# A two-direction Mamba block: direction 1's B taps read the projection in PSUM, every transpose goes through one bank, and ScalarE's state copy and two squares stand ahead of the square roots

## What is computed

```
o  = silu(dwconv3x3(lin1(x)))                    # 8 images, L = 256 positions
s  = o @ fc_in
for d in (0, 1):                                 # direction 1 works on the flipped sequence
    z, xBC, dt = split(s @ W_in[d])
    xBC = silu(causal_conv1d(xBC, 4 taps))       # xs, B, C of 16 channels each
    h_t = exp(-dt*A) * h_(t-1) + dt*xs_t (x) B_t # scan over the 256 positions
    y_t = h_t . C_t + D*xs_t
    y   = y * silu(z);  y = y * rsqrt(mean(y*y) + 1e-5) * norm_w
    out += y @ W_out[d]
o  = batchnorm(out @ fc_out);  x1 = sigmoid(conv4(o)) * x + x
... layer norm, causal attention, layer norm, top-2 of 8 experts, residual
```

## Time and profile before

| | |
|---|---|
| median of 3 runs | 89.81 us (89.72 to 90.68) |
| the profiled execution | 90.41 us |
| its span, first to last instruction | 88.6 us |
| outside the span | 1.81 us |
| TensorE / VectorE / ScalarE / GpSimd busy | 91% / 66% / 46% / 23% |
| TensorE's granted clock | full in all of the span |

### The profile page before, as it was taken

The page is one execution under the profiler, slowest core; times in us unless marked ns, Lnnn a source line. Parts: engine busy times, 40 slices in busy tenths (PEclk is TensorE's granted clock), DMA queues, the critical chain, the costliest instruction groups (busy, mean ns, idle before and its releaser), DMA issues.

```text
span 88.6 us, 1936 instructions
## 1 busy us (share of the span) xinstructions
PE 80.4 (91%) x734; PEld 52.3 (59%) x734; DVE 58.7 (66%) x153; ACT 40.6 (46%) x94; POOL 20.6 (23%) x31
## 2 busy tenths in 40 slices
PE   4899999999899999899489799999999899999790
PEld 1268775464665665346245566876756545789680
DVE  1149996999989999564644366529326969999210
ACT  4040297988738710567368762333753242001100
POOL 6050004998699107910000000000000000000000
DMA  2994000000000000000000000000000000001001
GB/s 19 367 435 167 0 0 0 0 0 0 7 0 4 0 7 0 4 7 0 0 0 0 0 0 7 0 0 0 0 7 0 0 0 0 0 7 33 30 0 59
DMA packets 1305, 2.57 MB, mean 29 GB/s; under 512 B 144, under 2 KB 784, under 8 KB 1296
## 3 DMA queue, kind: packets, MB, share of 16 engines
q1 hardware_dynamic: 1152, 2.31, 7.2%
q10 hardware_dynamic: 144, 0.14, 0.5%
HBM read 2.19 MB, written 0.26 MB: 28 GB/s over the span
## 4 chain that ended last, share of the span: by engine, by line
PE 52%; DVE 23%; ACT 12%; issue 6%; DMA 4%; ACTq 0%; DVEq 0%
PE banks L1006 7%; DVE lmat L1159 6%; DVE pre L1152 4%; DMA pa<-in_pa 4%; PE banks L675 3%; PE banks L929 3%; DVE conv L1090 3%; PE banks L974 3%; PE banks L754 2%; PE banks L581 2%; PE banks L692 2%; PE banks L913 2%; PE banks L897 2%; DVE lmat L1380 2%; PE banks L662 2%
## 5 line engine op out<-in xcount | busy, mean ns | idle before, releaser
L574 PE MATMUL banks<-warm 128*128 128x512 bf16 x36 | 10.9, 422 | 1.2 <-DVE warm L1072 1.2
L1159 DVE TENSOR_TENSOR_SCAN lmat<-banks,data 128x512 f32<-128x512 f32 x8 | 9.8, 1219 | 0.8 <-PE banks L675 0.7
L1006 PE MATMUL banks<-pa,lmat 128*128 128x128 f32 x56 | 6.8, 277 | 0.0
L1006 PEld LDWEIGHTS banks<-pa,lmat 128*128 128x128 f32 x56 | 6.5, 192 | 0.1
L574 PEld LDWEIGHTS banks<-warm 128*128 128x128 bf16 x36 | 3.4, 106 | 4.8 <-issue 1.4
L301 POOL TENSOR_TENSOR data<-pa,dt_dir 128x512 f32<-128x512 f32 x4 | 4.0, 1042 | 7.9 <-DVE da L1139 7.9
L1380 DVE TENSOR_TENSOR lmat<-banks,wtok 128x256 f32<-128x256 f32 (+1 forms) x12 | 5.5, 506 | 0.2
L974 PE MATMUL banks<-pd,h 32*128 32x256 f32 x32 | 5.2, 397 | 0.1
L1165 DVE TENSOR_TENSOR mmat<-banks,lmat 128x512 f32<-128x512 f32 x8 | 5.4, 669 | 0.0
L301 POOL TENSOR_TENSOR data<-pb,dt_dir 128x512 f32<-128x512 f32 x4 | 5.0, 1262 | 0.0
L510 ACT ACTIVATE data<-banks 128x384 f32<-128x384 f32 x8 | 3.4, 491 | 3.0 <-PE banks L913 2.9
(11 more groups left out here) (201 smaller groups left out, 178.2 us busy)
## 6 DMA issues: line engine op xcount, KB each, us to landing
pc<-in_pc SPq DMA_DIRECT2D x1, 962.5 KB, 5.8
pb<-in_pb SPq DMA_DIRECT2D x1, 446.0 KB, 3.9
pd<-in_pd SPq DMA_DIRECT2D x1, 336.0 KB, 6.2
x<-in_x SPq DMA_DIRECT2D x1, 256.0 KB, 3.2
out<-fin SPq DMA_DIRECT2D x4, 64.0 KB, 1.6
pa<-in_pa ACTq DMA_DIRECT2D x1, 133.5 KB, 3.4
```

What stands on the lines that cost most here:

```text
L574: pe.matmul(bank[scratch][:, :], warm[:, 0:P], warm[:, :], start=True, stop=True)
L1006: mm = pe.matmul(o, mix[:, k, e, :, :], packs["ident"], start=False, stop=(e == terms - 1))
L1159: dve.tensor_tensor_scan(lmat[:, i, :], dab_bank, data1[:, i, :, :].rearrange("p q t -> p (q t)"), 0.0, ALU.mult, ALU.add).then_inc(S["sca ...
```

## The change

- `raw_copy(2)` is gone. `tap(2, s)` reads projection 2 in PSUM bank 6, as `tap(0, s)` did with bank 2, and `raw` holds direction 1's C and z alone.
- Both directions are transposed into bank 1. `transposed(0)` waits for `raw_copy(3)`, and `transposed(1)` for direction 0's two turn copies.
- The six filler matmuls write bank 1 too, so they wait for these two turn copies. `skipped(0)`, the first writer of bank 6, also waits for the last tap.
- On ScalarE `state_copy(1, 0)` stands ahead of `rms(1)`, and `square(3)` ahead of `rms(2)`. On TensorE `mean_squares(3)` and `(4)` each stand one place further ahead of the mixer's matmuls.

```diff
-        raw = sb("raw", [P, DIRS, BH, L])
+        raw = sb("raw", [P, BH, L])
...
-        t_part = lambda d, bh: unit_bank[d][:, L * bh:L * bh + L]
+        t_part = lambda bh: unit_bank[1][:, L * bh:L * bh + L]
...
             def centre_tap(n):
                 if n == 3:
-                    act.wait_ge(S["raw_ready"], 2)
+                    act.wait_ge(S["raw_ready"], 1)
...
             centre_tap(0)
             centre_tap(2)
-            raw_copy(2)
...
             rms(0)
             square(1)
+            state_copy(1, 0)
             rms(1)
-            state_copy(1, 0)
             square(2)
             state_copy(1, 1)
+            square(3)
             rms(2)
-            square(3)
             square(4)
             rms(3)
             rms(4)
...
             def transposed(d):
                 pe.wait_ge(S["s1_ready"], d + 1)
-                pe.wait_ge(S["raw_ready"], d + 1)
+                if d == 0:
+                    pe.wait_ge(S["raw_ready"], 1)
+                else:
+                    pe.wait_ge(S["s1t_copied"], BH)
...
             def skipped(i):
                 pe.wait_ge(S["s1t_copied"], BH if u == 0 else BH * DIRS)
+                if u == 0:
+                    pe.wait_ge(S["tapped"], 2 * PAD)
...
             products(0)
-            pe.wait_ge(S["raw_ready"], DIRS)
+            pe.wait_ge(S["s1t_copied"], BH)
             keep_warm(6, 1)
...
+            mean_squares(3)
             mixer_out(0, 0)
-            mean_squares(3)
+            mean_squares(4)
             mixer_out(0, 1)
-            mean_squares(4)
             mixer_out(1, 0)
             keep_warm(1, 6)
             mixer_out(1, 1)
...
             def tap(n, s):
-                if n == 2:
-                    dve.wait_ge(S["raw_ready"], 1)
-                src = raw[:, 0, :, :] if n == 2 else proj[n]
+                src = proj[n]
```

More of the change, by code:

```diff
@@ L373, in centre_tap @@
                 if n == 3:
-                    act.wait_ge(S["raw_ready"], 2)
+                    act.wait_ge(S["raw_ready"], 1)
                 else:
                     act.wait_ge(S["proj_done"], PROJ_ORDER.index(n) + 1)
-                act.activation(pre[:, n, :, :], raw[:, 1, :, :] if n == 3 else proj[n], ACT.Copy,
+                act.activation(pre[:, n, :, :], raw[:, :, :] if n == 3 else proj[n], ACT.Copy,
                                scale=packs["tap_col"][:, TAPS1 * n + PAD:TAPS1 * n + TAPS1])\
@@ L382, in raw_copy @@
                 act.wait_ge(S["proj_done"], PROJ_ORDER.index(n) + 1)
-                act.activation(raw[:, n - 2, :, :], proj[n], ACT.Copy).then_inc(S["raw_ready"], 1)
+                act.activation(raw[:, :, :], proj[n], ACT.Copy).then_inc(S["raw_ready"], 1)
             def other_taps(n):
@@ L387, in other_taps @@
                     col = TAPS1 * n + PAD - s
-                    act.activation(tap3[:, s - 1, :, :], raw[:, n - 2, :, :], ACT.Copy,
+                    act.activation(tap3[:, s - 1, :, :], raw[:, :, :], ACT.Copy,
                                    scale=packs["tap_col"][:, col:col + 1]).then_inc(S["tap3_ready"], 1)
@@ L426, in turn_copy @@
                 act.wait_ge(S["s1t_done"], d + 1)
-                act.activation(s1t[:, d, NC * bh:NC * bh + NC, :, :].rearrange("p k q c -> p (k q c)"), t_part(d, bh),
+                act.activation(s1t[:, d, NC * bh:NC * bh + NC, :, :].rearrange("p k q c -> p (k q c)"), t_part(bh),
                                ACT.Copy).then_inc(S["s1t_copied"], 1)
@@ L643, in transposed @@
                 pe.wait_ge(S["s1_ready"], d + 1)
-                pe.wait_ge(S["raw_ready"], d + 1)
+                if d == 0:
+                    pe.wait_ge(S["raw_ready"], 1)
+                else:
+                    pe.wait_ge(S["s1t_copied"], BH)
                 for bh in range(BH):
                     for c in range(NC):
-                        mm = pe.transpose(t_part(d, bh)[:, Q * c:Q * c + Q], s1[:, d, bh, Q * c:Q * c + Q], packs["ident"])
+                        mm = pe.transpose(t_part(bh)[:, Q * c:Q * c + Q], s1[:, d, bh, Q * c:Q * c + Q], packs["ident"])
                 mm.then_inc(S["s1t_done"], 1)
```

## The result

The changed kernel took 89.9 us, the median of 21 executions (88.74 to 91.89), beside 90.52 us for the kernel before, run beside it (89.72 to 93.56, also 21). The ratio is 0.9889 (0.9856 to 0.9922), which at the 89.81 us shown is a gain of 1.00 us, to 88.8. The forecast was 88.7 with a range from 88.2 to 89.5, and the measured 89.9 lies above it. So the ratio bears out most of the gain, and the median does not: it lies 1.1 us above the ratio's time.

The account below looks back on a forecast made before the run. It took one dependent line across engines as the bound, with VectorE's taps bounding at 18 to 25 us. Terms 0.42 + 0.43 + 0.27 = 1.12 us, taken from 89.81, gave 88.7 us, range 88.2 to 89.5.

Parts of the forecast that it names:

- The taps at 0.75 each: VectorE's second three B taps, read from PSUM, take 0.75 us each, so scan(1) ends 0.95 us earlier.
- Place one: The stretch from 18 to 25 us, taps to decays(2): decays(2) starts 0.42 us earlier, TensorE-bound from there.
- place two: The stretch from 36 to 43 us, output_carry to last mixer matmul: 0.43 from state copy plus 0.27 us from squares.
- The fillers at 20.65, their new wait of no cost: TensorE's fillers before decays(2) still start at 20.65 us; their wait for the second turn copy costs 0.
- Rival A: Turn copies come late, fillers and decays(2) slip, and all 0.42 us is lost: 89.1 us, chance 0.12.
- The state copy 0.43: Moved ahead of rms(1) on ScalarE, it lets output_carry start without its wait: 0.43 us (0.39 to 0.47).
- the squares and mean squares 0.27: At the last roots, their new order brings the last normed piece and mixer matmul 0.27 us further forward.
- Rivals B: At the roots, late gated(3) holds rms(2); 0.27 and half of 0.43 us go: 89.2 us, chance 0.10.
- C: The PSUM source makes the taps longer, up to 1.405 us each, delaying scan(1): 90.1 us, chance 0.04.
- The copy removed ... is worth 0: Removing one 0.58 to 0.60 us copy from ScalarE gains 0, since ScalarE sits idle later anyway.
- the distance from it to the end unchanged: From the last mixer matmul to the kernel's end, everything moves along with no change in length.
- Rival D: TensorE's clock falls to 1.2 of 2.4 GHz between 30 and 44 us, adding 2 us: 90.7, chance 0.02.

Follow-up runs that it names:

- e4_lock: Kernel before, taps still from SBUF, with one added wait holding GpSimd's fifth step until the last B tap is over; ratio 0.9923.
- e2_taps: Changed kernel without the edits to the roots: taps from PSUM, one transpose bank and new waits alone; ratio 0.9967 to the kernel before.
- e5_state: Kernel before with only the state copy moved ahead of rms(1); ratio 0.9929.
- e3_roots: Kernel before with state copy, square(3) and mean squares moved as in the change; taps, banks and waits as before; ratio 0.9914.
- e8_spare: Changed kernel plus a 128x1 ScalarE copy into an unread tile where the removed copy stood; median 90.88 us of 6, no ratio.
- e13_before_late: Kernel before with three extra matmuls on unused data among the last four experts; median 93.81 us, ratio 1.0373.
- e11_late: Changed kernel with a spare ScalarE copy, four fillers instead of six, and three extra matmuls among the last four experts; median 95.25 us.
- e12_thin: Changed kernel with a spare ScalarE copy, four fillers instead of six, and two instead of six unused matmuls ahead of the last four experts; ratio 0.9804.

## Why the prediction was right in most of its parts and wrong in its number

- **The taps at 0.75 each.** Right: 2.29 us for three, GpSimd's instruction 1.04. The reading that the excess was a wait for GpSimd, taken from three end times, was borne out by e4_lock for all three taps. The surplus for a PSUM source that the Trainium skill gives (VectorE: DVE Perf Modes, the errata table) would have been, as an estimate from that table, 65 ns a tap; with GpSimd out of the way the two sources took 747 and 748 ns, so the trace doesn't agree here. The Trainium skill's advice that the prediction names, to copy to SBUF first where many operations follow (VectorE: DVE Perf Modes, "Rules for kernel authors"), is what the kernel before did, and it met what the Trainium skill's exclusion rule (SBUF — State Buffer, "SBUF: two separate sides") describes: e4_lock agrees with that rule, since a tap that began beside a GpSimd step ended 0.55 us behind the step's end and the taps without one took 748 ns.
- **Place one at 0.42 (0.35 to 0.51).** TensorE-bound from there on, as said, and without a wait ahead of decays(2). Measured 0.53, 0.59 and 0.53 with place two, and 0.41 alone; counted from the fillers' start, which takes out its own noise, 0.51 to 0.52 in all four (1.82 less 1.30 or 1.31), at the upper end. The step that was mis-sized is "decays(2) can start between 21.96 and 22.12; I take 22.05". In the trace after decays(2) starts 1.30 us behind the fillers' start, 0.17 ahead of their modelled end, where I had taken 1.40 and 0.07; before, an idle time stood behind the fillers, so this couldn't be read there.
- **The fillers at 20.65, their new wait of no cost.** Right: counted from the first tap they start at 6.00 after and at 6.01 before, and where they start at 6.11 (e2_taps) so they do in e5_state, which has the old wait. Rival A, that this wait eats the gain, fell.
- **The state copy 0.43, the squares and mean squares 0.27.** Right, the best two terms: e5_state gives 0.46 and e3_roots 0.26 more; both and 0.05 of interplay make 0.77. Rivals B and C fell.
- **"The copy removed ... is worth 0".** Wrong, and with it "the distance from it to the end unchanged". It cost 0.30 us at the gate, 30 us later; a spare instruction in its place takes that back (e8_spare), and with it moves a transfer of instructions from the gate to 35.25 us. How the one does the other isn't shown. This is the one term that was put at nothing and cost time; the sum would have been 0.42 + 0.43 + 0.27 - 0.30 = 0.82. Since the terms before it came out 0.18 larger (1.30 for 1.12), the measured 1.00 lies near the forecast for partly the wrong reason.
- **The clock.** This is the step that failed. Rival D, "the clock", had a chance of 0.02 because TensorE's new idle times were no longer than old ones; it looked only at 30 to 44 us, and the rest was taken over from one profile of the kernel before ("The full clock is granted throughout"). What came was a fall at 77 us, in a stage that keeps its instructions, in 6 of 27 executions, and it costs 1.6 us of the profiled one. I asked what the change does to TensorE where it stands, and not what an earlier arrival does to the stages behind it. Why an earlier arrival lets the clock fall stays open.
- **The basis.** "89.81 - 1.12" took the median of three. In 21 executions the same kernel had a median of 90.52. Leaving out on both sides the executions named in the result leaves 16 of before with a median of 90.05 and 11 of after with 89.07, which differ by 0.98. The number 89.9 is 89.07 plus what the other ten executions do to a median of 21: without the five with the fallen clock alone, the median of the other 16 is 89.38, inside the range. So the 1.21 us between 88.69 and 89.90 are 0.24 of a basis too low (90.05 for 89.81), 0.14 of a gain too large (1.12 for 0.98), 0.31 of the executions with a long first convolution and 0.52 of the fallen clock. Each of the first three would have fitted a range to 89.5, and so would their sum, 89.38; the clock's 0.52 did not.

## What to carry to other kernels

Where two instructions on VectorE and GpSimd overlap and one has an odd duration, test whether the odd one ends at a fixed distance behind the other's end before blaming the operand; holding one of them back by a semaphore (e4_lock) won as much at decays(2) as the rewrite of the taps alone (7.42 both) and more at the gate (0.48 us against 0.15). When an engine loses an instruction, compare the stages far behind it too: here one instruction less cost 0.3 us at a critical instruction 30 us later, and a spare one gave it back. Check an edit that is to make an engine's use denser by a count in its own trace: e13_before_late's made it thinner. And where a kernel runs TensorE near its limit, look at the granted clock of many executions, not of one: an edit can shorten the path in each and still take the clock from some.

## What the runs showed of the hardware that I had not expected

- A spare ScalarE instruction of 0.20 us made the path 0.32 us shorter (e8_spare, 31.49 to 31.17), together with an instruction transfer (33 GB/s in a quarter microsecond) that moved from 46.5 to 35.25 us.
- The granted clock can fall to half for some 3.4 us in mid-kernel while TensorE is busy, in some executions and not in others: within half a microsecond of the start of a dense group of fp32 matmuls in five profiles, and 4 us ahead of it, for 6.8 us, in e11_late. Three more bf16 matmuls among the experts' raised it from 0 of 74 to 5 of 6.
- Each of these three, 0.39 us long, made its stretch of TensorE 0.7 us longer (3.05 to 5.19 us), since the experts' matmuls between them took 0.28 us each instead of 0.19.
- The lowest ratio is that of e12_thin, 0.9804: two fillers less, a spare instruction, and four matmuls less ahead of the last experts. The clock still fell in four of its eight executions.
